# P x latents in fp32 with the latents stationary and P streamed, two heads on two column tiles, key sums on GpSimd

## The chip, the core and the metric

The kernel runs on one core of one Trainium2 chip. The metric is the device time of one execution in microseconds; the time of a version is the median of its runs.

## What is computed

A transformer layer over x of shape (16, 512, 256) in fp32: x plus attention plus feed-forward, both on the layer norm of x.

```python
q = (x @ Wq.T).reshape(b, t, 8, 64)
kv_latent = x @ Wkv_down.T                      # 64 wide
k = (kv_latent @ Wk_up.T).reshape(b, t, 8, 64)
v = (kv_latent @ Wv_up.T).reshape(b, t, 8, 64)
scores = einsum('bqhd,bkhd->bhqk', q, k) * 64 ** -0.5
out = einsum('bhqk,bkhd->bqhd', softmax(scores), v)
attn = out.reshape(b, t, 512) @ Wo.T

def fp4_linear(x, w):                           # blockwise FP4 rounding of both sides, blocks of 16
    return einsum('bsk,nk->bsn', fp4_quant_dequant(x), fp4_quant_dequant(w))
h = silu(fp4_linear(x, w_gate)) * fp4_linear(x, w_up)    # 704 wide
ffn = fp4_linear(h, w_down)
x = x + attn(layernorm(x)) + ffn(layernorm(x))
```

## The kernel before

Wq and Wk_up are multiplied together beforehand, and so are Wv_up and Wo (`wqk`, `wov`). A head then works on the 64 latents alone: its scores are q' x latents, and its output is P x latents, a 512 x 64 matrix, to which `wov` is applied.

The work goes in 128 slots: one for each of the 16 sequences and 8 heads. In the same slot the feed-forward runs for a quarter of the tokens (128) and one half of the 704 hidden columns, so an even slot t takes the first half and the odd slot t+1 the second. Each engine has its own program, written as `slot(t)`, and the order of the instructions in it is fixed by hand; they meet through semaphores. The first 16 slots and the last 16 are written out, the others are a hardware loop over two sequences. Before them stand 12 slots of weight preparation, behind them four slots of tail.

TensorE's slot (L914 to L1031): gate matmuls into bank `m0` (six of L779, each product as three fp32r matmuls of high and low parts), row scores `mx` (L868) of the head two slots ahead, from which only the row maximum is taken, a transpose of the row maxima (L933), the up matmuls into `m1`, transposed scores `st` (L894, L895) of the head itself, `turn_hidden` (three transposes L881), the down projection of the hidden part of two slots before (nine of L779, into `m0`), and at the end what comes once in a few slots: the latents, q of the next pair (odd slots), W_ov on the attention output (two slots in eight), transposes of the next x tokens (L1015, odd slots), of the attention output (L1021, even slots) and of the latents (L1029, one slot in eight).

P x latents is `weigh` (L897). P, in `probs` with keys on the partitions, is the stationary side in blocks of 128 keys x 128 queries; the streamed side is `lat_tok`, the 64 latents and a column of ones, so column 64 of the result is the sum over keys. It is called four times per slot, for the key blocks 2 and 3 of the head before and 0 and 1 of the head itself, and fills bank `po` with queries on the partitions. Everything in it is full fp32.

VectorE's slot (L636 to L760): statistics of the next x tokens (even slots), silu (L655), row maxima (L616), the low part of the turned hidden `ht_lo` (L662), `hid` (L667), block scales of `hid` (L588 to L593), then for the head before the reciprocal of the key sums (L680) and `on` (L685), which is `po` scaled by it, two more row maxima, the addition of the down projection to `acc` (L702), norm and scales of x (even slots), the rounding of h to the FP4 grid (`to_grid`: L598, L600, L602), q and x low parts (odd slots), W_ov's addition (L740), `on_lo` (L750, even slots) and the rounding of x (even slots).

GpSimd multiplies h and x by the block scales and subtracts the rounding constants (L416, L447, L456). ScalarE does tanh, the exponentials (L511) and copies of the high parts. TensorE's gate matmuls of the next slot wait for L702, since both use `m0`, and its next down projection waits for `ht_lo`; scores `mx` wait for the row maxima taken from their bank. Small DMAs of the maxima and the loads and stores of x go on SP's queue.

## Time and profile before

| | us |
|---|---|
| median of 3 runs | 1718.05 |
| lowest, highest | 1705.89, 1718.47 |
| the profiled execution | 1717.89 |
| its span (first to last instruction) | 1716.0 |
| TensorE busy | 1589.8 |
| VectorE busy | 1342.3 |
| ScalarE busy | 709.0 |
| GpSimd busy | 518.9 |

Busy time is the union of an engine's instructions. TensorE's matmuls overlap each other at their ends, so its share says little of how densely they are packed; the chain of waits and the timeline tell more. In all views PE is TensorE, PEld its weight loads, DVE VectorE, ACT ScalarE, POOL GpSimd. L909 is line 909 of the kernel.

### The profile page before, as it was taken

What the parts mean: (1) busy time and instruction counts of PE and PEld (TensorE: products, weight loads), DVE (VectorE), ACT (ScalarE), POOL (GpSimd) and SP (SyncE); (2) the same over time, 40 slices, a digit from 0 to 9 for tenths busy, and PEclk for the clock granted to TensorE, in tenths of its full rate; (3) what the DMA queues carried; (4) which work ended last, traced back from release to release, by engine and by line L of the source; (5) the groups of instructions that cost most, each with busy time, mean ns of one, the idle gap of its engine ahead of it and who ended that gap; (6) DMA issues with size and microseconds to landing.
All of it is one profiled execution on the core that took longest, in us unless ns stands there. A gap on an engine that the chain in (4) does not pass through costs nothing.

```text
span 1716.0 us, 33440 instructions
## 1 busy us (share of the span) xinstructions
PE 1589.8 (93%) x10726; PEld 1449.4 (84%) x10726; DVE 1342.3 (78%) x3368; ACT 709.0 (41%) x1382; POOL 518.9 (30%) x696
## 2 busy tenths in 40 slices
PE   1599999999999999999999999899998999999998
PEld 0488988989889898888989899898988989899897
DVE  7788887878878787788768878778887878887664
ACT  2444443443434443444443444344443444344432
POOL 7433232233323232232323323222323223222211
PEclk9799999999999999999999999999999999999999
DMA  3000000000000000000000000000000000000000
GB/s 97 10 7 4 14 14 7 17 8 20 4 10 20 5 20 7 12 14 8 17 9 20 4 14 13 6 20 7 10 14 10 17 7 20 4 14 8 1 14 13
DMA packets 22932, 23.11 MB, mean 13 GB/s; under 512 B 3280, under 2 KB 22224, under 8 KB 22736
## 3 DMA queue, kind: packets, MB, share of 16 engines
q1 hardware_dynamic: 22736, 20.65, 4.0%
q8 instruction: 104, 1.70, 0.4%
q14 instruction: 92, 0.75, 0.1%
HBM read 11.99 MB, written 8.39 MB: 12 GB/s over the span
## 4 chain that ended last, share of the span: by engine, by line
PE 82%; DVE 11%; issue 5%; ACT 1%; DMA 0%; DVEq 0%; POOL 0%; SPq 0%; ACTq 0%; POOLq 0%
PE m L779 34%; PE po L909 22%; PE mx L868 7%; PE st L894 6%; PE st L895 6%; PE m L881 2%; PE m L1015 2%; PE m L933 1%; DVE row_max L616 1%; PE m L1021 1%; DVE hid L600 1%; DVE on_lo L750 1%; PE m L1029 1%; DVE h_small L588 1%; ACT q_hi L551 1%
## 5 line engine op out<-in xcount | busy, mean ns | idle before, releaser
L909 PEld LDWEIGHTS po<-lat_tok,probs 128*128 128x128 f32 x4096 | 523.8, 194 | 23.0 <-DVE on L685 0.3
L909 PE MATMUL po<-lat_tok,probs 128*128 128x65 f32 x4096 | 519.5, 271 | 0.0
L511 ACT ACTIVATE probs<-st 128x512 f32<-128x512 f32 x512 | 291.2, 595 | 339.0 <-PE st L895 339.0
L616 DVE TENSOR_REDUCE row_max<-mx 128x1 f32<-128x512 f32 x512 | 327.8, 682 | 0.7 <-PE mx L868 0.6
L416 POOL TENSOR_TENSOR h_norm<-hid,h_small 128x352 f32<-128x352 f32 x128 | 101.1, 790 | 481.9 <-DVE h_small L593 481.9
L894 PE MATMUL st<-q_hi,lat 128*128 128x512 f32 x512 | 212.7, 415 | 0.0
L895 PE MATMUL st<-q_lo,lat 65*128 65x512 f32 x512 | 203.6, 398 | 0.0
L779 PE MATMUL m<-wgu_hi,xt_hi 128*128 128x352 f32 x512 | 195.4, 382 | 8.6 <-issue 8.4
L447 POOL TENSOR_TENSOR h_norm<-h_norm,hid 128x352 f32<-128x352 f32 x128 | 119.8, 936 | 216.9 <-DVE h_norm L602 216.9
L868 PE MATMUL mx<-lat,q_hi 128*128 128x512 f32 x512 | 179.0, 431 | 4.0 <-DVE row_max L616 3.9
L729 DVE TENSOR_TENSOR q_lo<-m,q_hi 64x512 fp32r<-64x512 f32 x128 | 88.1, 688 | 120.6 <-ACT q_hi L551 120.6
L551 ACT ACTIVATE q_hi<-m 64x512 fp32r<-64x512 f32 x256 | 151.6, 592 | 62.3 <-PE m L779 57.6
L779 PE MATMUL m<-wgu_lo,xt_hi 128*128 128x352 f32 x512 | 171.5, 335 | 0.0
L779 PE MATMUL m<-wgu_hi,xt_lo 128*128 128x352 f32 x512 | 170.5, 333 | 0.0
L531 ACT ACTIVATE ht_hi<-m 128x384 fp32r<-128x384 f32 x128 | 62.9, 491 | 196.3 <-PE m L881 196.3
L662 DVE TENSOR_TENSOR ht_lo<-m,ht_hi 128x384 fp32r<-128x384 f32 x128 | 71.2, 557 | 71.3 <-ACT ht_hi L531 71.3
L779 PEld LDWEIGHTS m<-wgu_hi,xt_hi 128*128 128x128 f32 x512 | 102.8, 201 | 27.7 <-issue 16.2
L519 ACT ACTIVATE hid<-m 128x352 f32<-128x352 f32 x128 | 59.5, 465 | 138.1 <-PE m L779 135.3
L779 PE MATMUL m<-wd_hi,ht_hi 128*128 128x256 f32 x384 | 107.3, 279 | 1.3 <-DVE ht_lo L662 1.3
L779 PE MATMUL m<-wd_hi,ht_lo 128*128 128x256 f32 x384 | 106.7, 278 | 0.0
L779 PE MATMUL m<-wd_lo,ht_hi 128*128 128x256 f32 x384 | 106.6, 277 | 0.0
L416 POOL TENSOR_TENSOR hq<-h_norm,h_small 128x352 f32<-128x352 f32 x128 | 101.0, 789 | 10.0
(178 smaller groups left out, 3063.7 us busy)
## 6 DMA issues: line engine op xcount, KB each, us to landing
x_in<-in_L_attn_x_dram SPq DMA_DIRECT2D x64, 128.0 KB, 2.1
out_dram<-acc SPq DMA_DIRECT2D x32, 256.0 KB, 2.2
q_lo<-neg_max SPq DMA_DIRECT2D x128, 2.0 KB
weights_in<-in_L_ffn_w_down_dram SPq DMA_DIRECT2D x1, 704.0 KB, 6.0
weights_in<-in_L_ffn_w_gate_dram SPq DMA_DIRECT2D x1, 640.0 KB, 4.5
acc<-in_L_ffn_w_up_dram SPq DMA_DIRECT2D x1, 640.0 KB, 5.6
wq_in<-in_L_attn_Wq_dram SPq DMA_DIRECT2D x1, 512.0 KB, 5.8
x_in<-in_L_attn_Wo_dram SPq DMA_DIRECT2D x1, 512.0 KB, 6.7
```

Of the source, the lines that this page charges most:

```text
L416: return pool.tensor_tensor(blocks(dst), blocks(src), per_block.unsqueeze(2).broadcast_to([rows, cols // BLOCK, BLOCK]), ALU.mult)
L447: pool.tensor_tensor(h_norm[:, :], h_norm[:, :], hid[:, w.c % 2, :], ALU.subtract).then_inc(h_grid, 1)
L511: act.activation(probs[:, t.c % 2, kc, :], st[kc % 2][:, :], ACT.Exp).then_inc(exp_done, 1)
L551: act.activation(q_hi[v * R:(v + 1) * R, 2 * m.c % QH + u, :], m1[u * R:(u + 1) * R, :], ACT.Copy).then_inc(q_hi_done, 1)
L616: dve.tensor_reduce(row_max[:, u.c % 2, qc:qc + 1], mx[qc % 2][:, :], AX.X, ALU.max).then_inc(mx_taken, 1)
L662: dve.tensor_tensor(ht_lo[:, u.c % 2, :, :], m2[:, 0:NB * P].rearrange("p (k q) -> p k q", k=NB), ht_hi[:, u.c % 2, :, :].bitcast(F32), AL ...
L729: dve.tensor_tensor(q_lo[0:R, h, :], m1[v * R:(v + 1) * R, :], q_hi[v * R:(v + 1) * R, h, :].bitcast(F32), ALU.subtract).then_inc(q_lo_don ...
L779: last = pe.matmul(dst, a, b, start=(n == 0), stop=(n == len(ms) - 1))
L868: pe.matmul(mx[qc % 2][:, :], q_hi[:, u.c % QH, qc * P:(qc + 1) * P], lat[:, s.c % 2, :], start=True, stop=True).then_inc(mx_psum, 1)
L894: pe.matmul(st[kc % 2][:, :], lat[:, s.c % 2, keys], q_hi[:, h, :], start=True, stop=False)
L895: pe.matmul(st[kc % 2][:, :], lat1[:, s.c % 2, keys], q_lo[:, h, :], start=False, stop=True).then_inc(st_psum, 1)
L909: last = pe.matmul(po[:, qc * P:qc * P + R + 1], probs[:, u.c % 2, kc, qc * P:(qc + 1) * P], lat_tok[:, s.c % 2, kc, 0:R + 1], start=(kc = ...
```

## The change

P x latents is turned round: the latents (128 keys x 64) are stationary, P is streamed with 512 queries, and the result has the 64 latents on the partitions. The two heads of a pair go to partitions 0 to 63 and 64 to 127 of `po`, that is to two column tiles of the array. It is done once per pair, at the start of the next even slot, and its result is already what the four transposes of `on` made before, so these go.

The streamed side has no column of ones any more. The sum over keys is made in two steps: GpSimd adds the four key blocks of P of each head (`add_keys`, three additions of 128x512), and TensorE sums over the partitions with 16 matmuls of one column (key sums stationary, the ones streamed), eight per head. VectorE takes the reciprocal of 128x8 values. They are stored to DRAM as a row per head, and loaded again spread over 64 partitions each (`inv_b`). VectorE multiplies `po` by it once per pair, in the odd slot. The high part of `on` is then ScalarE's copy from SBUF and the low part moves from VectorE to GpSimd. VectorE's rounding of h moves behind the q, x and W_ov parts of its slot. W_ov comes a slot later, and the tail has five slots.

In GpSimd's slot t, `add_keys(t - 1, 3)` and (even slots) `on_lo` stand first, `add_keys(t, 1)` and `add_keys(t, 2)` last. In VectorE's even slot the reciprocal stands first; `on` stands in the odd slot, in the place where it stood in every slot before.

```diff
         def wov_half(t):
 
             s = t.over(H).plus(-1)
-            m = s.times(2, t.c % H - 1)
-            return m if t.c % H in (1, 2) and m.within(B * 2) else None
+            m = s.times(2, t.c % H - 2)
+            return m if t.c % H in (2, 3) and m.within(B * 2) else None
...
+                m = weighed_pair(t)
+                if m is not None:
+                    sp.wait_ge(inv_done, m.n(1, 1))
+                    sp.dma_start(inv_rows[m.c % 2].rearrange("v (p j) -> (v p) j", p=R), inv_den[:, m.c % 2, :]).then_inc(inv_stored, 16)
...
+                if m is not None:
+                    sp.wait_ge(inv_stored, m.n(16, 16))
+                    for v in range(2):
+                        sp.dma_start(inv_b[v * R:(v + 1) * R, :],
+                                     inv_rows[m.c % 2, v:v + 1, :].broadcast_to([R, T])).then_inc(inv_spread, 16)
...
+            def add_keys(t, kc):
+                total, last = key_sum[:, t.c % 2, :], probs[:, t.c % 2, kc, :]
+                pool.wait_ge(exp_done, t.n(CH, kc + 1))
...
+                pool.tensor_tensor(total, first, last, ALU.add).then_inc(sum_step, 1)
...
+                    pool.wait_ge(on_hi_done, m.n(1, 1))
+                    pool.tensor_tensor(on_lo[:, m.c % PAIRS, :], on[:, :], on_hi[:, m.c % PAIRS, :].bitcast(F32),
+                                       ALU.subtract).then_inc(on_lo_done, 1)
...
+                    dve.wait_ge(den_psum, m.n(1, 1))
...
+                    dve.reciprocal(inv_den[:, m.c % 2, :], m2[:, 0:T // R]).then_inc(inv_done, 1)
...
-                    dve.reciprocal(inv, heads[:, :, R]).then_inc(inv_done, 1)
...
-                    dve.tensor_tensor(on[:, m.c % 2, :, v.c % 2 * R:(v.c % 2 + 1) * R], heads[:, :, 0:R],
-                                      inv.unsqueeze(2).broadcast_to([P, CH, R]), ALU.mult).then_inc(on_done, 1)
+                    dve.wait_ge(inv_spread, m.n(32, 32))
+                    dve.wait_ge(pv_done, m.n(CH, CH))
...
+                    dve.tensor_tensor(on[:, :], po[:, :], inv_b[:, :], ALU.mult).then_inc(on_done, 1)
...
-                    for qc in range(CH):
-                        last = pe.matmul(po[:, qc * P:qc * P + R + 1], probs[:, u.c % 2, kc, qc * P:(qc + 1) * P],
-                                         lat_tok[:, s.c % 2, kc, 0:R + 1], start=(kc == 0 and qc == 0),
-                                         stop=(kc == CH - 1), skip_group_check=True)
+                    for kc in range(CH):
+                        pe.wait_ge(exp_done, m.n(2 * CH, CH + kc + 1))
+                        for v in range(2):
+                            last = pe.matmul(po[v * R:(v + 1) * R, :], lat_tok[:, s.c % 2, kc, 0:R], probs[:, v, kc, :],
+                                             start=(kc == 0), stop=(kc == CH - 1))
+                        last.then_inc(pv_done, 1)
+                    m2_free(t.plus(-1))
+                    pe.wait_ge(sum_step, m.n(2 * (CH - 1), 2 * (CH - 1)))
+                    for j in range(T // R):
+                        for v in range(2):
+                            last = pe.matmul(m2[v * R:(v + 1) * R, j:j + 1],
+                                             key_sum[:, v, :].rearrange("p (q j) -> p q j", j=T // R)[:, :, j],
+                                             lat_tok[:, s.c % 2, 0, R:R + 1], start=True, stop=True)
+                    last.then_inc(den_psum, 1)
```

What this does to TensorE's order around the end of a pair. Before, from q of the next pair (`wqk`) at the end of an odd slot over the border to the even slot's gate matmuls (`po` is the bank of P x latents, `ident` marks transposes):

```order
L779 MATMUL m<-xt_hi,wqk_lo 128x512
L909 MATMUL po<-lat_tok,probs 128x65 x4
L1015 MATMUL m<-ident,xn 128x128 x2
L1015 MATMUL m<-ident,xq 128x128 x2
L909 MATMUL po<-lat_tok,probs 128x65 x4
L779 MATMUL m<-wgu_hi,xt_hi 128x352
```

The same place now:

```order
L830 MATMUL m<-xt_hi,wqk_lo 128x512
L1074 MATMUL m<-ident,xn 128x128 x2
L1074 MATMUL m<-ident,xq 128x128 x2
L964 MATMUL po<-probs,lat_tok 64x512 x8
L971 MATMUL m<-lat_tok,key_sum 64x1 x16
L830 MATMUL m<-wgu_hi,xt_hi 128x352
```

All of P x latents and the sums of a pair stand together there. The middle of a slot, between `turn_hidden` (`hq`) and the down projection (`wd`), was before:

```order
L881 MATMUL m<-ident,hq 128x128 x3
L909 MATMUL po<-lat_tok,probs 128x65 x4
L894 MATMUL st<-q_hi,lat 128x512
L895 MATMUL st<-q_lo,lat 128x512
L909 MATMUL po<-lat_tok,probs 128x65 x4
L868 MATMUL mx<-lat,q_hi 128x512 x2
L779 MATMUL m<-wd_hi,ht_hi 128x256
```

and is now:

```order
L937 MATMUL m<-ident,hq 128x128 x3
L950 MATMUL st<-q_hi,lat 128x512
L951 MATMUL st<-q_lo,lat 128x512
L924 MATMUL mx<-lat,q_hi 128x512 x2
L830 MATMUL m<-wd_hi,ht_hi 128x256
```

Two groups of four matmuls have left it. On GpSimd, from the multiplications by the scales in an even slot (`h_norm<-hid`, `x_norm<-xn`) to the subtractions in the odd slot, the order before is:

```order
L416 TENSOR_TENSOR h_norm<-hid,h_small 128x352
L416 TENSOR_TENSOR x_norm<-xn,x_small 128x256
L447 TENSOR_TENSOR h_norm<-h_norm,hid 128x352
L416 TENSOR_TENSOR hq<-h_norm,h_small 128x352
L456 TENSOR_TENSOR x_norm<-x_norm,xq 128x256
```

and now:

```order
L443 TENSOR_TENSOR h_norm<-hid,h_small 128x352
L443 TENSOR_TENSOR x_norm<-xn,x_small 128x256
L478 TENSOR_TENSOR key_sum<-probs 128x512
L478 TENSOR_TENSOR key_sum<-key_sum,probs 128x512 x2
L495 TENSOR_TENSOR h_norm<-h_norm,hid 128x352
L443 TENSOR_TENSOR hq<-h_norm,h_small 128x352
L504 TENSOR_TENSOR x_norm<-x_norm,xq 128x256
```

The three additions of the even slot's head stand between `x_norm` and the subtraction that ends the rounding of h.

## Rows read from the trace of the kernel before

**Rows 1.** The page's first part: busy time, share of the span, instructions.

```profile
PE 1589.8 (93%) x10726; PEld 1449.4 (84%) x10726; DVE 1342.3 (78%) x3368; ACT 709.0 (41%) x1382; POOL 518.9 (30%) x696
```

**Rows 2.** Chain of waits, 786 to 815 us: start, length, what.

```profile
788.89 1.03 PE m L779 x9
...
795.88 0.42 issue
...
798.51 0.84 PE po L909 x8
...
801.24 1.03 PE m L779 x9
...
804.04 0.44 PE m L1021 x4
...
811.40 1.03 PE m L779 x9
```

**Rows 3.** Timeline, VectorE and GpSimd: start, length, engine, line, out<-in, idle before.

```profile
799.55 0.51 DVE L667 TENSOR_TENSOR hid<-hid,m 128x352 f32<-128x352 f32 x1
...
804.37 0.28 DVE L598 TENSOR_SCALAR hid<-h_norm 128x352 uint32<-128x352 uint32 x1
804.60 0.62 POOL L416 TENSOR_TENSOR x_norm<-xn,x_small 128x256 f32<-128x256 f32 x1 [2.57 <-DVE x_small L593]
804.68 0.73 DVE L600 TENSOR_SCALAR hid<-hid 128x352 f32<-128x352 f32 x1
805.45 0.53 DVE L602 TENSOR_TENSOR h_norm<-h_norm,hid 128x352 f32<-128x352 f32 x1
...
807.08 0.79 POOL L416 TENSOR_TENSOR hq<-h_norm,h_small 128x352 f32<-128x352 f32 x1
807.19 0.83 DVE L600 TENSOR_SCALAR xq<-xq 128x256 f32<-128x256 f32 x1
...
808.40 0.51 DVE L655 SCALAR_TENSOR_TENSOR hid<-hid,m 128x352 f32<-128x352 f32 x1
...
810.03 0.55 DVE L662 TENSOR_TENSOR ht_lo<-m,ht_hi 128x384 fp32r<-128x384 f32 x1
...
814.40 0.34 DVE L600 TENSOR_SCALAR hid<-hid 128x352 f32<-128x352 f32 x1
```

**Rows 4.** Groups of instructions: busy us, mean ns of one, idle before.

```profile
L909 PE MATMUL po<-lat_tok,probs 128*128 128x65 f32 x4096 | 519.5, 271 | 0.0
...
L447 POOL TENSOR_TENSOR h_norm<-h_norm,hid 128x352 f32<-128x352 f32 x128 | 119.8, 936 | 216.9 <-DVE h_norm L602 216.9
...
L531 ACT ACTIVATE ht_hi<-m 128x384 fp32r<-128x384 f32 x128 | 62.9, 491 | 196.3 <-PE m L881 196.3
...
L456 POOL TENSOR_TENSOR x_norm<-x_norm,xq 128x256 f32<-128x256 f32 x64 | 47.1, 736 | 79.4 <-DVE x_norm L602 79.4
```

**Rows 5.** Timeline of TensorE, weight preparation: two fp32 blocks of 256 columns.

```profile
53.67 1.92 PE L827 MATMUL st<-weights_in 128*128 128x256 f32 x4
55.38 1.90 PE L827 MATMUL po<-weights_in 128*128 128x256 f32 x4
```

**Rows 6.** Two stretches: us, busy time of PE, PEld, DVE, ACT, POOL, granted clock, DMA.

```profile
53.67:55.30 1.63, 1.63 (x5) 1.35 (x5) 0.17 (x1) 0.60 (x1) 0.90 (x2) 0.50 0.00 0
265.30:272.20 6.90, 6.15 (x24) 5.75 (x25) 3.08 (x8) 1.12 (x3) 3.08 (x4) 0.51 0.01 2
```

**Rows 7.** Timeline, VectorE and GpSimd, weight preparation.

```profile
25.62 0.62 POOL L416 TENSOR_TENSOR weights_in<-on,h_small 64x256 f32<-64x256 f32 x1
25.72 0.79 DVE L602 TENSOR_TENSOR x_norm<-x_norm,xq 128x256 f32<-128x256 f32 x1
```

**Rows 8.** DMA issues: KB each, us from issue to landing.

```profile
out_dram<-acc SPq DMA_DIRECT2D x32, 256.0 KB, 2.2
```

**Rows 9.** Waits: who for whom, us in total, times, longest.

```profile
PE m L1029 <- DVE on_lo L750: 31.3, 15, 2.2
```

More of the change, by code:

```diff
@@ L262, in ltok_seq, with weighed_pair, scaled_pair, split_pair @@
             return s if t.c % H == 6 and s.within(B) else None
-        def turned_pair(t):
+        def weighed_pair(t):
             m = t.plus(-2).over(2)
             return m if t.c % 2 == 0 and m.within(B * PAIRS) else None
+        def scaled_pair(t):
+            m = t.plus(-3).over(2)
+            return m if t.c % 2 and m.within(B * PAIRS) else None
+        def split_pair(t):
+            return weighed_pair(t.plus(-2))
         def wov_half(t):
             s = t.over(H).plus(-1)
-            m = s.times(2, t.c % H - 1)
-            return m if t.c % H in (1, 2) and m.within(B * 2) else None
+            m = s.times(2, t.c % H - 2)
+            return m if t.c % H in (2, 3) and m.within(B * 2) else None
         LEAD = [At(c) for c in range(-12, 0)]
-        TAIL = [At(SLOTS + c) for c in range(4)]
+        TAIL = [At(SLOTS + c) for c in range(5)]
         def lead_slots(slot):
@@ L438, in weights @@
                     times_blocks(w[0:rows, :], ratio, w_small[q % 4][0:rows, 1, 0:cols // BLOCK]).then_inc(wq_done, 1)
+            def add_keys(t, kc):
+                total, last = key_sum[:, t.c % 2, :], probs[:, t.c % 2, kc, :]
+                pool.wait_ge(exp_done, t.n(CH, kc + 1))
+                if kc == 1:
+                    if t.over(2).any():
+                        pool.wait_ge(den_psum, t.over(2).n())
+                    first = probs[:, t.c % 2, 0, :]
+                else:
+                    pool.wait_ge(sum_step, t.n(CH - 1, kc - 1))
+                    first = total
+                pool.tensor_tensor(total, first, last, ALU.add).then_inc(sum_step, 1)
             def slot(t):
                 w = t.plus(-1)
+                if w.within(SLOTS):
+                    add_keys(w, 3)
+                m = split_pair(t)
+                if m is not None:
+                    pool.wait_ge(on_hi_done, m.n(1, 1))
+                    pool.tensor_tensor(on_lo[:, m.c % PAIRS, :], on[:, :], on_hi[:, m.c % PAIRS, :].bitcast(F32),
+                                       ALU.subtract).then_inc(on_lo_done, 1)
                 if w.within(SLOTS):
@@ L480, in slot @@
                     weights(t, 1)
+                if t.within(SLOTS):
+                    add_keys(t, 1)
+                    add_keys(t, 2)
             lead_slots(slot)
@@ L507, in exp @@
                         act.wait_ge(st_psum, t.n(CH, kc + 1))
[L509 to L510 removed]
+                        if t.over(2).any(CH, kc + 1 - CH):
+                            act.wait_ge(pv_done, t.over(2).n(CH, kc + 1 - CH))
+                        if kc == 0 and t.any(CH - 1, 1 - CH):
+                            act.wait_ge(sum_step, t.n(CH - 1, 1 - CH))
                         act.activation(probs[:, t.c % 2, kc, :], st[kc % 2][:, :], ACT.Exp).then_inc(exp_done, 1)
+                m = split_pair(t)
+                if m is not None:
+                    act.wait_ge(on_done, m.n(1, 1))
+                    if m.over(PAIRS).any(2):
+                        act.wait_ge(wov_psum, m.over(PAIRS).n(2))
+                    act.activation(on_hi[:, m.c % PAIRS, :], on[:, :], ACT.Copy).then_inc(on_hi_done, 1)
                 if t.within(SLOTS):
@@ L715, in slot @@
                     scales(xn[:, b, :], x_small[:, b, :, :], x_scales, n)
-                if t.within(SLOTS):
-                    dve.wait_ge(h_norm_done, t.n(1, 1))
-                    to_grid(h_norm[:, :], hid[:, t.c % 2, :], h_round, t)
                 s = lat_seq(t)
@@ L746, in slot @@
                                       xt_hi[:, v, :, c * P:(c + 1) * P].bitcast(F32), ALU.subtract).then_inc(xt_lo_done, 1)
-                m = turned_pair(t)
-                if m is not None:
-                    dve.wait_ge(on_hi_done, m.n(1, 1))
-                    dve.tensor_tensor(on_lo[:, m.c % PAIRS, :], m2[:, :], on_hi[:, m.c % PAIRS, :].bitcast(F32),
-                                      ALU.subtract).then_inc(on_lo_done, 1)
                 s = ltok_seq(t)
@@ L757, in slot @@
                                       ALU.add).then_inc(ltok_done, 1)
+                if t.within(SLOTS):
+                    dve.wait_ge(h_norm_done, t.n(1, 1))
+                    to_grid(h_norm[:, :], hid[:, t.c % 2, :], h_round, t)
                 if n is not None:
@@ L1017, in slot @@
                     last.then_inc(xt_psum, 1)
-                if m is not None:
-                    pe.wait_ge(on_done, m.n(2, 2))
-                    for c in range(CH):
-                        last = pe.transpose(m2[:, c * P:(c + 1) * P], on[:, m.c % 2, c, :], ident[:, :])
-                    last.then_inc(on_psum, 1)
                 if s is not None:
-                    if m is not None:
-                        pe.wait_ge(on_lo_done, m.n(1, 1))
                     pe.wait_ge(lat_lo_done, s.n(1, 1))
```

75 lines of the change are left out of this document (35 added, 40 removed).

## The prediction

> **What bounds the kernel now.** I read the page first [rows 1]: TensorE is busy for 93% of the span, VectorE for 78%, GpSimd for 30%. That names TensorE, but says nothing of what happens once TensorE has less to do, so I read on in time. The steady part is 64 pairs of slots, an even slot and the odd one behind it, and I cut a pair at its two down projections (nine matmuls of L779 in a row). In the chain of waits [rows 2] they start at 788.89 (odd), 801.24 (even) and 811.40 (odd): 10.16 us from even to odd (call it stretch A) and 12.35 us from odd to the next even (stretch B), 22.5 us for a pair without W_ov or latent work. Both are TensorE work almost without a gap: four groups of L909 at 0.84 us stand in each.
>
> How far is VectorE from being the bound? In the timeline of stretch A [rows 3] it starts `hid` (L667) at 799.55, ends the two rounding chains at 808.40 and writes `ht_lo` at 810.03 to 810.58. TensorE starts the down projection that needs it at 811.40. So VectorE has only some 0.8 us to spare in A, and the reader should see this beside the 93%: four groups of L909 and one of L1021 (4 x 0.84 + 0.44 = 3.8 us) are what TensorE does while VectorE catches up.
>
> **What leaves and what comes on TensorE, per pair.** L909 has 4096 instructions [rows 4] for 2048 matmuls in the code, so a full fp32 matmul is two instructions; eight of them take 0.84 us [rows 2], 0.105 each. Leaving: 64 x 0.105, or eight groups of 0.84, 6.7 us; and four transposes of `on`, 0.44 us [rows 2].
>
> Coming, first P x latents: eight matmuls of 512 columns, 16 instructions. The nearest row is L827, fp32 with 256 columns: the next block starts 1.71 us after the four instructions do [rows 5], 0.43 us each, at a granted clock of 0.50 [rows 6], the 1.2 GHz level. That is two cycles a column, so 512 columns at 2.4 GHz are 0.43 us an instruction. One after another the 16 take 6.8 us. If the two column tiles work at once, 3.4. The queue holds them as A A B B, and with TensorE starting in order only each A-B border overlaps, which gives nine steps of 0.43: 3.84 us. I take that. No row shows two tiles at once.
> The Trainium skill (TensorEngine Tiling (Array Packing), When to Use Tiling) recommends this very swap with two column tiles where the streamed side has at most 64 columns; no run here shows it. By its ideal factor of two it would be 3.4 us; if it did not hold, the serial rival below.
>
> Second, the denominators: 16 matmuls of one column, 32 instructions, each with a weight load of 64 columns. L909 is paced by its load of 128 columns at 0.105 us [rows 2]; half of that is 0.053, so 1.7 us in series, 0.85 if the tiles overlap, 3.4 if a short or strided load costs as much as L909's. I take 0.06 each, 1.9 us. TensorE's own sum per pair is then -7.1 + 5.7 = -1.4 us.
>
> **What comes on GpSimd, and what it does to VectorE.** Three additions of 128x512 per slot and one `on_lo` per pair. GpSimd's two-tensor subtraction takes 936 ns at 352 columns and 736 at 256 [rows 4]; 2.08 ns more per column makes 1.27 us at 512. That is (384 + 64) x 1.27 = 569 us on top of 519, about 63% of the span: GpSimd is not full. But see which VectorE instructions meet it. In [rows 3] L600 on `hid` takes 0.73 us while GpSimd has `x_norm` in work until 805.22, and 0.83 on `xq` with `hq` in work until 807.87; alone it takes 0.34 on `hid`. Each ends 0.15 to 0.2 us after GpSimd's instruction. L602, a tensor_tensor with both inputs in SBUF, takes 0.79 us for 256 columns at 25.72 beside GpSimd's 25.62 to 26.24, against 0.53 for 352 columns alone at 805.45 [rows 3, 7]. So a rounding instruction of VectorE is held until GpSimd's current one ends.
> The Trainium skill (SBUF — State Buffer, Who interferes with whom) says this as an exclusive lock on a shared port pair, for the fast modes and for two SBUF inputs. The trace agrees by the rows above. It is the rule that speaks against this change: without it stretch A below would be 4.1 us shorter.
>
> Stretch A after the change, counted on VectorE from `hid` (799.55 = 0), since it loses its cover. The on/inverse pair before the row maxima goes (some 0.5 us), so rounding of h starts at 804.37 - 799.55 - 0.5 = 4.3. L598 and L600, held by `x_norm` as now, end at 5.4. In GpSimd's queue three additions now stand behind `x_norm`, and then L447's subtraction. The four rounding instructions left (L602 on h; L598, L600, L602 on x) each get in only behind one of these: 5.2 (the end of `x_norm`, 805.22, on this count) + 3 x 1.27 + 0.94 + some 0.6 for handing over = 10.55. Today they and `on_lo` take 805.45 to 808.40, 2.95 us; now 5.15, although `on_lo` has left. From there to the end of `ht_lo` 2.2 us as now (808.40 to 810.58), and the down projection starts at 12.85. A grows from 10.16 to 12.85. TensorE's own work there is 10.16 - 3.8, of which all but the last row scores is done, after a wait of 1.4 us for `acc`, at about 7.3. It then waits for VectorE's first row maximum (10.55 + 1.1), some 4.3 us.
>
> Stretch B stays TensorE's: 12.35, minus four groups of L909 (3.36), minus the 0.42 us in which TensorE waited at 795.88 [rows 2], plus 3.84 + 1.9, plus a new wait. From the end of `turn_hidden` to the down projection is 798.51 to 801.24, 2.73 us; without two groups of L909 1.05 are left, while ht_hi (0.49) [rows 4], ht_lo (0.55) [rows 3] and three hand-overs of some 0.15 need 1.5. That is +0.46. B = 12.35 - 3.36 - 0.42 + 5.74 + 0.46 = 14.77.
>
> Waits that I cost at nothing. Inverse rows out to DRAM and back: two landings of the 2.2 us that a store takes [rows 8], hidden since `on` comes 10 us later; uncovered, up to 5 us a pair. On SP's queue the store stands ahead of the next row of maxima and the two loads behind it; SP's wait for the store thus delays only the loads of x and the stores behind, which have slots of slack. `on_lo` on GpSimd holds the rounding of h in B for 1.2 us, but the reciprocal behind it waits for the denominators anyway. The reciprocal of key sums blocks VectorE's queue (stats, silu) while TensorE has nothing for it.
>
> **Sum.** A pair: 12.85 + 14.77 = 27.6 against 22.5, +5.1; four pairs +20.4 per sequence. Back come: the W_ov work of an even slot (24 matmuls like the nine that take 1.03 us [rows 2], 2.75 us), which falls into the new wait of A but for about 1 us, -1.7; the latent work likewise, -0.7; and the wait of L1029 on `on_lo`, 2.15 us in 15 of 16 sequences [rows 9], goes together with the low clock behind it. In 265.3 to 272.2 the granted clock is 0.51 [rows 6], directly after such a wait: half-speed work of 6.9 us loses up to 3.4; I take 2.65 for it, so -4.8. Leaves +13.2. Against it stands the same effect: waits of 4.3 us are longer than those 2.15, so I expect the 1.2 GHz level behind three of four pairs, at 1.4 us lost each (bounds 0 and 2.7), +4.2. Together +17.4 per sequence, times 15.5 (of 16, the first and last are cut short) = +270. The tail adds about 6: both DRAM trips and the slower subtraction are uncovered for the last pair. 1718 + 270 + 6 = 1994; I say 1990. The profiled execution is 1717.9 us (span 1716.0) and the median 1718.05, so no shift is needed.
>
> **Rivals.**
> VectorE is not held and the end is faster. If GpSimd's additions don't hold the rounding, its six instructions take some 2.1 us at the lengths that they have alone, and A is 4.3 + 2.1 + 2.3 = 8.7 us, the pair 23.5; per sequence 4 x 1.0 - 7.2 = -3.2, no low clock: 1718 - 50 + 6 = 1674. It decides as soon as the rounding chains end before about 7.3. For it: GpSimd keeps a third of the span free, and its additions could come at other moments. Against it: its queue puts them right behind `x_norm`. TensorE's own sum of -1.4 us per pair (down to -2.9 at the low bounds) is behind this case too.
> The tiles do not overlap. P x latents takes 6.8 instead of 3.84, all of it on B: 62 x 3.0 = +185, 2180.
> The clock stays up: 1994 - 65 = 1930. The waits may be cut by small matmuls.
> Only fast-mode instructions are held, not tensor_tensor: 2.2 us less per pair in A, +4.4 per sequence, 1792 with the clock up, some 1850 with it down. Against it: L602 at 25.72.
>
> **How the numbers follow.** Forecast 0.42; clock up 0.12; half held 0.10; serial tiles 0.16; VectorE free 0.14; something near the old time, where gains and new waits cancel, 0.06. The range is 1760 to 2200: it leaves out the faster and the near-equal case and a little above serial tiles with the dear denominators. Faster by over 1% 0.15, within 1% 0.05, slower by over 1% 0.80; 1% is about what a measurement of this kernel can tell from no change.
>
> **What would show it.** In the timeline, the three rounding lines (L651, L653, L655 of the new file) at 1.2 us and more in even slots, each ending just behind a key sum; the longest wait of TensorE before `mx` in odd slots, for row_max, at 4 us; clock tenths under 9 in many slices; L964's 16 instructions in about 3.8 us with neighbours of two tiles overlapping; L971's 32 in 1.9. Wrong would be the theory if the rounding lines keep the lengths that they have alone in [rows 3] (0.34 and 0.53), or if TensorE's waits are under 1 us a pair; the serial case shows as 6.8 us of L964.

## The result and the profile after

| | before | after |
|---|---|---|
| median | 1716.83 us (1705.89 to 1718.47, 4 runs) | 2011.67 us (2008.54 to 2017.1, 4 runs) |
| ratio, 95% interval | | 1.1754 [1.1686, 1.1822] |
| span of the profiled execution | 1716.0 | 2010.0 |
| mean granted clock in it | 0.969 | 0.909 |

The change costs 295 us, 4.6 us for each of the 64 pairs. The ratio of each experiment below is to runs of the kernel before that were made beside it, and two of those, slow ones at 1968 and 1970 us with a granted clock of 0.747, are not counted in it. In this part line numbers are those of the kernel that is spoken of; one that has lines added or taken out is a few lines off the changed kernel.

First the page of the changed kernel, busy time by engine and its clock row (answering to [rows 1]):

```profile
PE 1616.5 (80%) x9446; PEld 1220.2 (61%) x9446; DVE 1552.4 (77%) x3176; ACT 692.7 (34%) x1382; POOL 1090.9 (54%) x1144
PEclk9788998988989999989989989889988989989998
```

TensorE is busy for 27 us more than before with 1280 fewer instructions, but this is now 80% of a longer span. VectorE is busy for 210 us more although 192 instructions left it. Who waited for whom says the same; the columns are us in total, times, longest:

```profile
PEld mx L924 <- DVE row_max L669: 304.5, 130, 6.4
PE mx L924 <- DVE row_max L669: 254.3, 64, 6.0
...
POOL on_lo L488 <- ACT on_hi L573: 160.1, 62, 6.4
```

TensorE waits once a pair, 4.0 us on the mean, for a row maximum. The third row, GpSimd waiting for ScalarE's high part of `on`, matters further down. The place of TensorE's wait is the end of stretch A. Here it is in the timeline of the changed kernel, VectorE and GpSimd, in the order of their starts, against [rows 3] of before:

```profile
939.67 0.51 DVE L727 TENSOR_TENSOR hid<-hid,m 128x352 f32<-128x352 f32 x1
...
943.93 0.28 DVE L651 TENSOR_SCALAR hid<-h_norm 128x352 uint32<-128x352 uint32 x1
944.16 0.62 POOL L443 TENSOR_TENSOR x_norm<-xn,x_small 128x256 f32<-128x256 f32 x1 [2.02 <-DVE x_small L646]
944.25 0.73 DVE L653 TENSOR_SCALAR hid<-hid 128x352 f32<-128x352 f32 x1
944.74 1.39 POOL L478 TENSOR_TENSOR key_sum<-probs 128x512 f32<-128x512 f32 x1
945.01 1.50 DVE L655 TENSOR_TENSOR h_norm<-h_norm,hid 128x352 f32<-128x352 f32 x1
946.20 2.77 POOL L478 TENSOR_TENSOR key_sum<-key_sum,probs 128x512 f32<-128x512 f32 x2
946.43 1.36 DVE L651 TENSOR_SCALAR xq<-x_norm 128x256 uint32<-128x256 uint32 x1
947.83 1.30 DVE L653 TENSOR_SCALAR xq<-xq 128x256 f32<-128x256 f32 x1
948.93 0.97 POOL L495 TENSOR_TENSOR h_norm<-h_norm,hid 128x352 f32<-128x352 f32 x1
949.16 1.03 DVE L655 TENSOR_TENSOR x_norm<-x_norm,xq 128x256 f32<-128x256 f32 x1
```

Read it as a ladder: each rounding instruction of VectorE from L653 on ends 0.2 to 0.4 us after one of GpSimd's, and the next one starts right behind it and is held again. Six roundings take from 943.93 to 950.19, 6.3 us; before they took 804.37 to 808.40, 4.0 us, with `on_lo` among them.

Then TensorE's rows around the wait, from its timeline (the down projections open with `wd_hi`):

```profile
922.16 1.40 PE L924 MATMUL mx<-lat,q_hi 128*128 128x512 f32 x2 [5.28 <-DVE row_max L669]
923.36 0.52 PE L830 MATMUL m<-wd_hi,ht_hi 128*128 128x256 f32 x1
...
939.90 0.36 PE L830 MATMUL m<-wd_hi,ht_hi 128*128 128x256 f32 x1 [0.33 <-DVE ht_lo L722]
...
951.28 1.39 PE L924 MATMUL mx<-lat,q_hi 128*128 128x512 f32 x2 [4.46 <-DVE row_max L669]
952.47 0.52 PE L830 MATMUL m<-wd_hi,ht_hi 128*128 128x256 f32 x1
```

Stretch B is 923.36 to 939.90, 16.54 us; stretch A 939.90 to 952.47, 12.57. This A is one without W_ov or latent work. Over 56 pairs (the first and the last sequence left out, each stretch measured between the first matmuls of two down projections in TensorE's timeline) A has a mean of 12.55 us before and 13.23 after, B 12.92 before and 16.79 after. So most of the loss, 3.9 us of 4.6 a pair, stands in B. And the chain of waits of the changed kernel through stretch B (start, length, what; [rows 2] before):

```profile
923.56 2.02 PE m L830 x9
925.58 0.43 PE st L950
...
929.35 3.58 PE po L964 x16
932.93 0.14 issue
933.07 2.09 PE m L971 x32
...
937.84 0.23 PE st L950
```

The down projection behind the wait takes 2.02 us for the nine matmuls that took 1.03 before, and a step of the scores 0.43 where it takes 0.23 at 937.84. The weighing takes 3.58 us, the denominators 2.09. The table of stretches gives the clock there (columns as in [rows 6]):

```profile
923.30:928.90 5.60, 5.60 (x22) 4.84 (x22) 3.52 (x9) 1.20 (x2) 3.62 (x4) 0.61 0.00 0
```

The granted clock is 0.61 over 5.6 us in which TensorE never stops, 1.1 us behind the wait of 5.28 us that ended at 922.16. It lies between the two levels, nearer to 1.2 GHz.

### The profile page after: what moved, and what is told of

Same layout as the page of the kernel before. It is cut to its first block, busy times and chain, and to the rows that moved or that the text cites. A ratio compares the mean times of both kernels' runs of the same rounds, so it can differ in the third digit from the quotient of the medians.

```text
span 2010.0 us, 32215 instructions
## 1 busy us (share of the span) xinstructions
PE 1616.5 (80%) x9446; PEld 1220.2 (61%) x9446; DVE 1552.4 (77%) x3176; ACT 692.7 (34%) x1382; POOL 1090.9 (54%) x1144
## 4 chain that ended last, share of the span: by engine, by line
PE 56%; DVE 29%; issue 11%; ACT 3%; DVEq 1%; POOL 0%; DMA 0%; SPq 0%; ACTq 0%; POOLq 0%
PE m L830 25%; PE po L964 10%; PE m L971 6%; PE mx L924 5%; DVE hid L653 4%; DVE row_max L669 4%; PE st L950 3%; PE st L951 3%; DVE xq L653 3%; DVE hid L651 3%; DVE xq L651 2%; ACT ht_hi L592 2%; DVE hid L715 2%; DVE h_small L641 1%; PE m L1074 1%
## 5 line engine op out<-in xcount | busy, mean ns | idle before, releaser
L924 PE MATMUL mx<-lat,q_hi 128*128 128x512 f32 x512 | 204.2, 476 | 256.1 <-DVE row_max L669 254.3
L478 POOL TENSOR_TENSOR key_sum<-key_sum,probs 128x512 f32<-128x512 f32 x256 | 331.4, 1295 | 35.8 <-ACT probs L564 15.0
L924 PEld LDWEIGHTS mx<-lat,q_hi 128*128 128x128 f32 x512 | 102.3, 207 | 310.1 <-DVE row_max L669 304.5
L964 PE MATMUL po<-probs,lat_tok 128*64 128x512 f32 x1024 | 233.8, 598 | 0.1
L830 PE MATMUL m<-wgu_hi,xt_hi 128*128 128x352 f32 x512 | 189.5, 370 | 26.3 <-DVE acc L758 14.6
L488 POOL TENSOR_TENSOR on_lo<-on,on_hi 128x512 fp32r<-128x512 f32 x64 | 82.2, 1284 | 160.1 <-ACT on_hi L573 160.1
L478 POOL TENSOR_TENSOR key_sum<-probs 128x512 f32<-128x512 f32 x128 | 167.0, 1305 | 0.0
L971 PEld LDWEIGHTS m<-lat_tok,key_sum 128*64 128x64 f32 x2048 | 130.2, 215 | 54.6 <-issue 48.6
L830 PE MATMUL m<-wd_hi,ht_hi 128*128 128x256 f32 x384 | 140.7, 366 | 27.7 <-DVE ht_lo L722 26.6
L964 PEld LDWEIGHTS po<-probs,lat_tok 128*64 128x64 f32 x1024 | 67.8, 136 | 121.7 <-issue 120.9
L971 PE MATMUL m<-lat_tok,key_sum 128*64 128x1 f32 x2048 | 131.3, 257 | 5.9 <-issue 0.8
```

Source lines behind the costliest of these rows:

```text
L478: pool.tensor_tensor(total, first, last, ALU.add).then_inc(sum_step, 1)
L830: last = pe.matmul(dst, a, b, start=(n == 0), stop=(n == len(ms) - 1))
L924: pe.matmul(mx[qc % 2][:, :], q_hi[:, u.c % QH, qc * P:(qc + 1) * P], lat[:, s.c % 2, :], start=True, stop=True).then_inc(mx_psum, 1)
L964: last = pe.matmul(po[v * R:(v + 1) * R, :], lat_tok[:, s.c % 2, kc, 0:R], probs[:, v, kc, :], start=(kc == 0), stop=(kc == CH - 1))
L971: last = pe.matmul(m2[v * R:(v + 1) * R, j:j + 1], key_sum[:, v, :].rearrange("p (q j) -> p q j", j=T // R)[:, :, j], lat_tok[:, s.c % 2, ...
```

## The experiments

The theory: VectorE's roundings, held by GpSimd's additions, make stretch A longer; TensorE's weighing and denominators make stretch B longer; the waits bring the low clock. The rivals are those of the prediction.

### Take the additions' length away, and put them into the kernel before

```diff
-                total, last = key_sum[:, t.c % 2, :], probs[:, t.c % 2, kc, :]
+                total, last = key_sum[:, t.c % 2, 0:16], probs[:, t.c % 2, kc, 0:16]
```

The key sums of the other 496 queries are left out (they stay at one).

> The changed kernel with GpSimd's key sums made over 16 of the 512 queries (the others stay one, so the sums are left out for them); number, order and waits of all instructions stay. Theory (VectorE's rounding is held by GpSimd's long additions): the rounding instructions fall back to about 0.33, 0.34 and 0.53 us, TensorE's waits for row_max from 254 us to under 60, stretch A by 4 us, the granted clock rises to 0.96 or more, and the time falls from 2012 to about 1700 (1640 to 1760). Rival (what is lost is TensorE's cover and the lump at the start of an even slot, whoever adds): the time stays above 1900.

Measured: 1798.38 us, 1.0469 [1.0439, 1.05] of before. So 213 of the 295 us go with the length of the additions, but 81 stay: less was gained than expected. The mean of A falls from 13.23 to 10.66 us, that of B from 16.79 to 16.07. The roundings are not free yet; the rows of groups show how far (busy, mean ns). `h_norm` is as it is alone, but `x_norm` takes twice the 460 ns of the kernel before, beside GpSimd's subtraction for h, and the first rounding instruction on `hid` 823 ns against 309. In stretch B of the changed kernel that one starts at 932.75 and ends at 934.08, 0.2 us behind `on_lo`, which the change gave to GpSimd:

```profile
L659 DVE TENSOR_TENSOR h_norm<-h_norm,hid 128x352 f32<-128x352 f32 x128 | 67.3, 526 | 4.4
L659 DVE TENSOR_TENSOR x_norm<-x_norm,xq 128x256 f32<-128x256 f32 x64 | 61.2, 957 | 2.2
L655 DVE TENSOR_SCALAR hid<-h_norm 128x352 uint32<-128x352 uint32 x128 | 105.4, 823 | 1.5 <-POOL h_norm L444 0.9
```

The other way round, the kernel before with the three additions per slot as GpSimd's extra work that nobody reads:

```diff
             def slot(t):
+                    add_keys(w, 3)
...
+                    add_keys(t, 1)
+                    add_keys(t, 2)
```

> The kernel before, with the same three additions per slot put into GpSimd's queue in the same places and their result unused. Theory: the same hold on VectorE without any change on TensorE. The rounding chains end some 2.9 us later in an even slot, 0.8 of it is free, so stretch A grows by 2 to 3 us: 1850 to 1920, with some low clock. Rival (GpSimd has room at 30% busy, only the new place of P x latents matters): at most 1735.

Measured: 1825.04 us, 1.0625 [1.0601, 1.0648]. The additions alone cost 107 us, 1.7 us a pair, with nothing else of the change there but ScalarE's wait for them before it overwrites P, which is not among its larger waits. The last rounding instruction on `h_norm`, L622, has gone from 526 ns to 1466:

```profile
L622 DVE TENSOR_TENSOR h_norm<-h_norm,hid 128x352 f32<-128x352 f32 x128 | 187.6, 1466 | 4.4
```

The rival that VectorE is not held falls with both. The cost is smaller than the 1850 to 1920 expected; a likely reason, not tested, is that TensorE has its old groups of L909 to do meanwhile.

### One head after the other on the column tiles

```diff
-                    for kc in range(CH):
-                        for v in range(2):
+                    for v in range(2):
+                        for kc in range(CH):
```

> The changed kernel with P x latents issued as four key blocks of the first head and then four of the second, the same 16 instructions. Theory (the two tiles work at once only where a matmul of one tile follows one of the other in the queue): one border instead of eight, so L964 takes 6.4 to 6.8 us a pair instead of 3.6, all of it on stretch B: 2012 + 62 x 3.0 = about 2190 (2150 to 2220). Rival (the 3.6 us come from a faster fp32 stream, not from two tiles at once): 2012 within 1%.

Measured: 2089.22 us, 1.217 [1.2144, 1.2196], 78 us over the changed kernel and below the 2150 to 2220 expected. In the chain the weighing runs from 930.38 to 935.73, with two denominators of 0.12 us among it:

```profile
930.38 4.00 PE po L967 x13
934.38 0.12 PE m L975
934.50 0.49 PE po L967 x2
935.00 0.12 PE m L975
935.14 0.59 PE po L967
```

That is 5.1 us of weighing against 3.58. The two tiles do work at once, and alternating them is worth 1.5 us a pair; but even head by head it is not the 6.8 us of a serial run. In the program all denominators stand behind the whole weighing; here two of them start ahead of its last instructions, so TensorE does not keep the program's order between the two tiles. 1.2 us a pair reached the end of the kernel.

### Fill TensorE's wait

```diff
+                    for _ in range(4):
+                        last = pe.matmul(po[0:32, :], hq[:, 0, HALF:NB * P], wq_in[:, 0:2, :]..., start=False, stop=True)
                 query_scores(t, 2)
```

> The changed kernel with four added matmuls of zeros (32 columns stationary, 512 streamed, fp32, about 3.4 us) in odd slots, put where TensorE waits for row_max, accumulated into po. Theory (the wait lets the clock fall to its 1.2 GHz level and the work behind it pays): the granted clock rises from 0.909 to above 0.95, and the time falls by 60 to 110 us, 1900 to 1950, though TensorE has 210 us more to do. Rival (the low clock costs nothing, since VectorE sets the pace): 2012 or above.

Measured: 1970.8 us, 1.1464 [1.1427, 1.1502]. Work that is added for nothing makes the kernel 41 us faster; the mean granted clock goes from 0.909 to 0.965, and the nine matmuls behind the wait take 1.28 us instead of 2.02. The same stretch B in both kernels, the changed one first (columns as in [rows 6]):

```profile
923.40:939.90 16.50, 16.03 (x96) 11.68 (x96) 10.86 (x25) 6.63 (x13) 8.08 (x8) 0.87 0.02 7
```

```profile
923.10:937.70 14.60, 14.14 (x95) 10.04 (x96) 11.24 (x25) 6.50 (x13) 8.11 (x8) 1.00 0.04 8
```

At a granted clock of 1.00 it is 1.9 us shorter. On the mean of 56 pairs B falls from 16.79 to 15.86 us and A, which holds the filler, rises from 13.23 to 13.52: one of its groups takes 3.6 us for eight instructions, 0.44 each. The low clock thus costs some 0.9 us a pair or more, an estimate from these means, of which the filler gives a third back.

### Move the additions, move the denominators, or both

The additions of a head go one slot later, behind GpSimd's `xq` and ahead of its `h_norm`:

```diff
-                    add_keys(w, 3)
                 m = split_pair(t)
...
+                    for kc in range(1, CH):
+                        add_keys(w, kc)
                 n = norm_chunk(t)
```

> The changed kernel with GpSimd's three key-sum additions of a head moved from behind x_norm (where they run beside VectorE's roundings) to the next slot, behind GpSimd's xq and ahead of its h_norm, where it was idle for 2.0 to 4.0 us. The work on every engine stays the same, only its place. Theory (VectorE's roundings were held by the additions that ran beside them): the roundings on hid, xq, h_norm and x_norm fall back to a mean under 0.6 us, TensorE's wait for row_max under 100 us of the 254, the time to 1820 us (1770 to 1870), near the 1798 of the short additions. Rival (the additions cost by their load on GpSimd or on memory, wherever they stand): still 1950 or more. Second rival (GpSimd, now late with h_norm, sets the end of a slot): 1880 to 1950, with the row_max wait gone and VectorE waiting for h_norm instead.

Measured: 2424.17 us, 1.4154 [1.4111, 1.4197], by the letter the first rival's "1950 or more", but for a reason that neither had. The waits name a ring that I had not seen:

```profile
PE m L969 <- POOL key_sum L478: 469.3, 64, 8.1
...
POOL on_lo L486 <- ACT on_hi L571: 283.5, 63, 10.1
```

In GpSimd's in-order queue the additions now stand behind `on_lo` and the subtraction of h. `on_lo` waits for ScalarE's `on_hi`, which stands behind its copies of q. TensorE had the denominators at the very start of the slot, so it stood still for 7.3 us in each pair, and with it all that feeds GpSimd. Stretch A did come down as the theory says (10.78 us on the mean instead of 13.23; the longest wait for the row maximum is 3.5 us instead of 6.0, in all 104.5 instead of 254.3); B paid for it. Of the roundings, `h_norm` is free (526 ns), but the last two of x, beside the subtraction of h, and the first on `hid`, beside `on_lo`, stay at 826 to 935 ns, above the 0.6 us expected.

Then the denominators alone. They leave `weigh` and stand behind the even slot's down projection on TensorE, and the reciprocal behind the addition to `acc` (L758) on VectorE:

```diff
                                        for k in range(NB)]).then_inc(down_psum, 1)
+                denominators(t)
...
                     dve.tensor_tensor(a, m0[:, 0:D], before, ALU.add).then_inc(down_taken, 1)
+                m = weighed_pair(t)
+                if m is not None:
+                    dve.wait_ge(den_psum, m.n(1, 1))
```

> The changed kernel with the 32 small matmuls of the denominators moved from the start of an even slot to behind its down projection, where TensorE waits for VectorE anyway, and the reciprocal behind the acc addition. Theory (in the stretch from an odd to an even slot TensorE's own chain of weighing and denominators sets the time, 3.58 and 2.09 us): 2.1 to 2.2 us less in each of 64 pairs, some 130 us, so 1880 us (1850 to 1920). Rival (VectorE's chain, held by GpSimd, sets that stretch, and TensorE's extra work there is covered): within 1.5% of 2012. Second rival: the key sums' last addition or the two DMA trips of the reciprocals are late now, and on waits for inv_b: above 2012.

Measured: 1965.14 us, 1.1462 [1.1425, 1.1499]: 47 us of the 130, which fits neither the theory's range nor a rival's. On the mean of 56 pairs B falls by 1.9 us, from 16.79 to 14.89, nearly the 2.1 expected, but A rises by 1.2, from 13.23 to 14.43. The timeline of VectorE shows one part of what A pays:

```profile
921.04 0.41 DVE L749 TENSOR_TENSOR acc<-m,x_in 128x256 f32<-128x256 f32 x1
922.03 0.21 DVE L756 RECIPROCAL inv_den<-m 128x8 f32<-128x8 f32 x1 [0.58 <-PE m L973]
922.21 0.41 DVE L763 TENSOR_SCALAR xn<-x_in,mean_var,rstd 128x256 f32<-128x256 f32 x1
```

I had put the reciprocal ahead of `xn`, where it waits for the denominators and starts the roundings, which set A, 0.76 us later. The other 0.4 us was not traced.

And both edits in one kernel:

> Both moves at once. Theory (two independent costs in two different stretches): the two gains add, 2012 - 190 - 130, 1690 us (1620 to 1760), which would be at or below the kernel before (1717). Rival (the second gain needs the first, or both hide the same time): no better than the better of the two alone, 1800 or more.

Measured: 1918.45 us, 1.1204 [1.1161, 1.1246]. The gains do not add. With the denominators out of the slot's start the ring is open, but TensorE still waits for the additions (60.3 us in 44 waits), and `rstd`, which `xn` needs, now stands behind all three. How much each of the two costs was not measured.

### Round h where it was rounded before

```diff
+                if t.within(SLOTS):
+                    dve.wait_ge(h_norm_done, t.n(1, 1))
+                    to_grid(h_norm[:, :], hid[:, t.c % 2, :], h_round, t)
                 s = lat_seq(t)
```

(and the same three lines taken out behind `ltok`).

> The changed kernel with one part undone: VectorE rounds h ahead of q_lo and xt_lo again, as in the kernel before, instead of behind them. Theory (the roundings are held by GpSimd's instructions wherever they stand): within 2% of 2012. Rival (the later place of h's rounding is what costs): 1950 or less, with VectorE's wait for the chunk's transposes instead of the row_max wait.

Measured: 1952.54 us, 1.1397 [1.136, 1.1435]. This place costs 59 us, although the roundings themselves are held longer than ever (the mean on `h_norm` is 1500 ns). The time is outside the theory's 2% and 2.5 us above the rival's "1950 or less"; TensorE's wait for the row maxima fell to 105.7 us but did not go, so the rival is right in what it says costs the time, and not in the sign that it names. A wait in the changed kernel shows part of the mechanism, with the same wait in this one below:

```profile
DVE acc L793 <- PE m L830: 38.6, 17, 5.6
```

```profile
DVE acc L796 <- PE m L830: 8.6, 2, 5.5
```

In two slots of eight VectorE has to add the W_ov product. In the changed kernel the rounding of h stands behind this addition, so VectorE first waits for TensorE's 24 W_ov matmuls and then rounds, with TensorE waiting in turn. With the rounding ahead, VectorE works while TensorE does W_ov. Here is the stretch A with W_ov in the changed kernel, 14.01 us long:

```profile
968.18 0.36 PE L830 MATMUL m<-wd_hi,ht_hi 128*128 128x256 f32 x1 [0.33 <-DVE ht_lo L722]
...
974.13 0.69 DVE L793 TENSOR_TENSOR acc<-m,acc 128x512 f32<-128x512 f32 x1 [1.83 <-PE m L830]
974.74 1.12 DVE L651 TENSOR_SCALAR hid<-h_norm 128x352 uint32<-128x352 uint32 x1
...
982.19 0.49 PE L830 MATMUL m<-wd_hi,ht_hi 128*128 128x256 f32 x1
```

In two of the other three stretches A of a sequence the low part of the latents (`lat`) and `lat_tok` stand ahead of the rounding in the same way. In the changed kernel the four A have medians of 14.00, 13.75, 13.43 and 12.57 us; with the rounding ahead they are all at 12.56 to 12.66. On the mean A falls by 0.8 us and B by 0.3.

### The same work in an order that avoids all of it

GpSimd: one addition ahead of `h_norm` in the odd slot, five behind `hq` in the even slot, `rstd` ahead of them, `on_lo` behind `h_norm`. VectorE: h rounded ahead of `q_lo`, the reciprocal behind the scales of x. TensorE: denominators behind the even slot's down projection.

> All of the changed kernel's work, in another order. GpSimd: the additions stand only where it was idle and VectorE does not round (one ahead of h_norm in an odd slot, five behind hq in an even slot), rstd ahead of them, on_lo behind h_norm; VectorE rounds h ahead of q_lo again; the denominators stand behind the even slot's down projection, their reciprocal behind the scales of x. Theory (what the change costs is the hold of the roundings, GpSimd's queue, and the denominators' place; the weighing itself is near the 3.36 us it replaces): roundings under 0.6 us each, 1760 us (1700 to 1830). Rival (the amount of work is what costs, TensorE's 2.1 us of denominators and GpSimd's 9.1 us per pair, in any order): 1860 or more. It differs from both_moved in that GpSimd's additions no longer wait for on_hi and h_norm no longer waits for them; if it does not fall below 1860 that account of the 1918 is wrong.

Measured: 1839.65 us, 1.0746 [1.0727, 1.0766], between the theory's 1830 and the rival's 1860. The roundings are at 0.32 to 0.59 us; what is left is a new wait:

```profile
PE m L978 <- POOL key_sum L476: 95.8, 46, 3.6
```

With that kernel, half as many and wider denominators:

```diff
-                    for j in range(T // R):
-                        for v in range(2):
-                            last = pe.matmul(m2[v * R:(v + 1) * R, j:j + 1], key_sum[:, v, :]...[:, :, j],
+                    for v in range(2):
+                        for j in range(CH):
+                            last = pe.matmul(m2[:, v * CH + j:v * CH + j + 1], key_sum[:, v, :]...[:, :, j],
```

> The kernel e3_reordered with the denominators in 8 matmuls of 128 stationary columns instead of 16 of 64 on two column tiles (the trace counts 16 instead of 32), so that half the instructions do the same sums. Theory (each of these costs 65 ns whatever it holds, and TensorE's chain sets the pair): 16 x 0.065, 1.0 us less on TensorE in each of 64 pairs, up to 65 us less than e3_reordered. Rival (VectorE's chain sets the pair and TensorE waits there anyway): less than 15 us.

Measured: 1972.96 us, 1.1524 [1.1503, 1.1545], 133 us slower than its parent, all of it in stretch A (15.96 us on the mean against 13.88). The premise was wrong. The chain of the parent and of this one, and the loads of another pair of this one:

```profile
905.60 2.02 PE m L978 x32
```

```profile
934.32 3.89 PE m L978 x16
```

```profile
733.38 3.81 PEld L978 LDWEIGHTS m<-lat_tok,key_sum 128*128 128x128 f32 x16
```

A step with 64 stationary columns on one of two tiles costs 0.063 us, one with all 128 columns 0.243. The clock is not the reason: the granted clock is 0.65 in the pair at 934.4 and 1.00 in the one at 733.65 to 737.20, and both take about as long. Nor can it be the width alone, for L909 before loaded 128 columns in 0.105 us. Those lay side by side; here a load takes every fourth column of the key sums, in the parent every eighth. The distance between the columns is the likelier cause, but it was not tried apart.

Last, GpSimd's queue spread again: two additions in the odd slot, ahead of and behind its `h_norm`, and two ahead of and two behind `rstd` in the even one:

```diff
+                if t.c % 2:
+                    if w.within(SLOTS):
+                        add_keys(w, 1)
+                else:
+                    if t.plus(-2).within(SLOTS):
+                        add_keys(t.plus(-2), 3)
+                    if w.within(SLOTS):
+                        add_keys(w, 1)
...
+                if t.c % 2 == 0 and w.within(SLOTS):
+                    add_keys(w, 2)
+                    add_keys(w, 3)
...
+                if t.c % 2 and w.within(SLOTS):
+                    add_keys(w, 2)
```

> The kernel e3_reordered with GpSimd's queue spread once more: two of the six additions of a pair in the odd slot (ahead of and behind its h_norm) instead of one, and rstd between the first two and the last two of the even slot. In e3_reordered TensorE waited 106 us for the last addition before the denominators. Theory (that wait was on the path): it falls below 40 us and the time to 1775 us (1740 to 1815). Rival (another chain is as late): 1820 or more.

Measured: 1713.74 us (10 runs), 0.9993 [0.997, 1.0016] of before, 26 us below the low end of what was expected. Page and waits of this kernel, to be held against those of the changed one above:

```profile
PE 1571.4 (92%) x9446; PEld 1195.6 (70%) x9446; DVE 1362.5 (79%) x3176; ACT 693.0 (40%) x1382; POOL 1079.5 (63%) x1144
```

```profile
PEld mx L929 <- DVE row_max L675: 38.5, 57, 3.9
```

The instruction counts are those of the changed kernel on every engine, and GpSimd's busy time is nearly the same. VectorE's is 190 us less, and the wait of TensorE's weight loads for the row maxima fell from 304.5 to 38.5 us. So the whole loss can be undone by order alone. Which of the moves brings which part is not told, as they were made together.

> The changed kernel's order with the weighing as it is, but without the denominators: no key sums on GpSimd, no small matmuls, no reciprocals, no transfers of them; on is multiplied by a constant. It leaves out the division by the sum of the weights. The theory (the denominators with their key sums cost all of the loss, and the weighing with the latents stationary next to nothing): the 1798 of the short additions less 64 x 2.1 us of TensorE, 1665 us (1620 to 1725), at or below the kernel before. Rival (weighing on two column tiles is itself slower, or on_lo on GpSimd and the later rounding of h hold VectorE by themselves): 1760 or more.

Measured: 1699.2 us, 0.9911 [0.9878, 0.9944]. Without the sums the order of the changed kernel is 1% faster than before. This lies in the theory's range. So the weighing itself, turned round, costs nothing that shows; the sums cost 313 us where the change put them and 15 us in the last order, as far as the two kernels, whose other order differs too, can be compared. No kernel here beats the one before by more than 1%; the only one that is faster leaves work out.

## Why the prediction was right

The forecast was 1990 us, the time 2011.67. Step by step:

- **Stretch A, held roundings: right.** From the start of `hid` I had the rounding of h at 4.3 and the end of all roundings at 10.55; the rows say 943.93 - 939.67 = 4.26 and 950.19 - 939.67 = 10.52. A is 12.57 against 12.85 forecast, TensorE's wait 4.0 us on the mean against 4.3. One part of this is luck. The 12.85 are counted from the start of `hid`, the 10.16 before from the down projection, and before these two stood 1.69 us apart (799.55 and 801.24). In the changed kernel they are 0.23 apart, since the down projection of the even slot now waits for `ht_lo`, right ahead of `hid`. The prediction has this wait in B but does not say that it needs it for A. On its own count the down projection came at 12.80. The two opposed experiments (213 us away with short additions, 107 us come in the kernel before) show it as a cause. The sentence of the Trainium skill on VectorE and GpSimd (SBUF — State Buffer, Who interferes with whom) holds for the rows here: the kinds that it names are the held ones, `q_lo`, `row_max` and `acc`, which read PSUM, keep their lengths (688, 673 and 415 ns on the mean, against 688, 682 and 415 before).
- **P x latents: mechanism right, size high by a little.** I counted nine steps of 0.43 us, as if only neighbours of different tiles overlapped, 3.84; measured 3.58, nearly the 3.4 of two full tiles. Head by head shows the overlap to reach further than the borders: 5.1 us, not near the 6.8 of the serial rival. The premise that TensorE starts in the program's order does not hold between the tiles. Rival out.
- **Denominators: 1.9 forecast, 2.09 measured.** But the reason that I gave, half of L909's load of 128 columns, was luck: with the columns apart a full-width step costs 0.243 us and not 0.105. Half of that is some 0.12 for 64 columns, an estimate, and two tiles at once make 0.065 of it. I had half the price and no overlap.
- **Additions: 1.27 forecast, 1.30 measured; GpSimd 63% forecast,** and 54% of a longer span measured, 1091 us against 1088.
- **Stretch B: mechanism right, 1.8 us short.** 14.77 forecast, 16.54 measured. The 14.77 are without the low clock, for which I put 1.4 us on three of four pairs, and this is the term that was mis-sized. Here nine matmuls of the down projection take 0.99 us more than before and four of the score steps 0.20 more each (0.43 against 0.23), 1.8 us in all, and at a granted clock of 1.00, with the filler, the same stretch takes 14.6 us. The clock rival is out: it stays low, and the filler gets 41 us back.
- **W_ov falls into the wait of A, -1.7: near, 1.4.** The A with W_ov was 2.9 us longer than the one without before (medians 13.04 and 10.17) and is 1.4 longer now (14.00 and 12.57). With the rounding of h ahead of W_ov's addition it is nothing (12.57 in both). I read the move of the rounding in the diff and costed it at nothing. It costs 59 us.
- **The sum of a sequence.** I had +17.4 us, of it 3.6 in the four A (all that comes back is put there) and 13.9 in the four B (with the clock). The means give +2.7 and +15.5, together +18.2. (The wait of L1029 is 31.3 / 15 = 2.09 us in the rows, not 2.15, which changes the sum by less than 0.1.) So the forecast was near in both stretches. B's 1.6 us too little lie in the clock, as far as the one stretch above tells. In A the place of the rounding of h, 3.1 us a sequence that I left out, is hidden by other terms that were too high by 4.0 together: there the nearness is in part luck.
- **Costed at nothing: the DRAM trips.** They land in 1.4 and 2.9 us, and no wait for `inv_b` is among the larger ones: right.
- **What I expected of the experiments** was less good than the forecast. It treated the 295 us as two separate sums, one for A and one for B. The two moves together gave 93 us, not 320; moving the additions alone cost 412. Each engine's queue couples the stretches.

## What to carry over

A queue on an idle engine is not free: GpSimd had 46% of the span left, but its additions stood exactly beside VectorE's SBUF roundings and four of the six in a pair's ladder took 1.0 to 1.5 us instead of 0.3 to 0.5. Before giving work to GpSimd, list what VectorE runs in the same microseconds, and place the work beside its PSUM reads or its waits. Before moving an instruction in any in-order queue, write down what then stands ahead of it and whom that waits for: the same instructions in four of the orders tried took 1714, 1840, 2012 and 2424 us.

## What the runs showed of the hardware beyond that

- A fp32 matmul step with one streamed column costs 0.063 us with 64 stationary columns and two column tiles in turn, 0.243 us with 128 columns and one tile (2.02 us for 32, 3.89 for 16), the latter at a granted clock of 0.65 as at 1.00. Whether the width or the distance between the stationary columns does it was not tried apart; 128 columns side by side took 0.105.
- Two column tiles given in turn take 3.58 us for 16 instructions of 512 columns, one head after the other about 5.1; the filler's, on one tile of 32 columns, take 0.44 each.
- Eight instructions of pure filler in a 4 us wait made the kernel 2% faster, with the mean granted clock up from 0.909 to 0.965.
